# Attention's q and k projected transposed, with halves exchanged by ScalarE, and V summed out of a double-width product

## The chip, the cores and the metric

The kernel runs on one core of a Trainium2 chip. A core has five engines that work side by side, each through its own list of instructions in order: TensorE (PE: matrix products and transposes into PSUM, a memory of eight banks), VectorE (DVE), ScalarE (ACT), GpSimd (POOL) and SyncE (SP, which issues transfers). They wait for one another by semaphores. The metric is the device time of one execution in microseconds (us).

## The reference

A "macaron" layer over x, 8 batches of 1024 rows of 128 values: half a feed-forward, attention, half a feed-forward. The feed-forward is a mixture of 16 experts. The change lies in attention:

```python
    x = x + 0.5 * _L0_ffn_ref(_layernorm(x, axis=-1), ...)
    x = x + _L0_attn_ref(_layernorm(x, axis=-1), w_q, w_k, w_v)
    x = x + 0.5 * _L0_ffn_ref(_layernorm(x, axis=-1), ...)

def _rotate(t, cos, sin):
    te = t[..., 0::2]
    to = t[..., 1::2]
    re = te * cos + to * sin
    ro = -te * sin + to * cos
    return jnp.stack((re, ro), axis=-1).reshape(t.shape)

def _L0_attn_ref(x, w_q, w_k, w_v):
    q = jnp.einsum('bmd,ed->bme', x, w_q)
    ...
    q_rot = _rotate(q, cos, sin)
    k_rot = _rotate(k, cos, sin)
    scores = jnp.einsum('bqd,bkd->bqk', q_rot, k_rot) / jnp.sqrt(d)
    scores = jnp.where(causal[None], scores, -jnp.inf)
    attn = jax.nn.softmax(scores, axis=-1)
    return jnp.einsum('bqk,bkd->bqd', attn, v)
```

## The kernel before

**Precision.** Most products are taken in the type fp32r, and for them an operand is split into a high part (`_h`, a copy that rounds) and a low part (`_l`, value minus high part), and three products are added: high x high, high x low, low x high (`mm3`). The product of the probabilities with V is in plain fp32 and shows as two instructions for each block of 128 x 128.

**Stages.** Each feed-forward runs over 16 tiles of 512 rows; in a tile, `j` counts 9 units, each with two `mm3` (gate and up) and, three units later, a down product. POOL makes the low part of h for the down product (`low_half`, L385). Attention runs over 8 batches. A batch goes through 8 steps, one for each block of 128 rows: in step i PE issues the scores of block i+1, the product of the probabilities of block i-1 with V, and the transposes of the probabilities of block i. DVE takes the row maximum (`attn_max`), ACT the exponential (`attn_exp`, L692) and the copies of transposed probabilities, DVE adds the result to X (`attn_residual`, L1176).

**The projections of the next batch** are woven into these steps by a table, `STEP_ITEMS`. An item `xnT` transposes normalized x (ACT copies the high part xh, DVE subtracts for xl). An item `qkv` (eight in a batch, one for each 128 rows) multiplies 128 rows of x with the 384 columns of all three weights; ACT copies the product to `qkv_both`. POOL rotates q and k with rows on partitions: times cos, times sin with neighbouring columns exchanged, and their sum `rot` (L482, L473, L488), each 128x256. An item `qkT` (four in a batch) transposes two blocks of `rot` on PE (L1544); ACT copies the high part, DVE subtracts for the low one (L1158). Items use PSUM banks 5 and 7 in turn, and PE waits until the item before last has left its bank. Layer norm of the batch after next is made by DVE in steps 1 to 3 (`attn_ln`), POOL (`attn_shift`, L461 to L465) and ACT in steps 4 to 7 (`attn_xn`, L569).

**The first batch** has no attention batch before it. Its projections are woven into the last tile of the first feed-forward, tile 15, by `FIRST_STEPS` (PE), `SIN_STEPS` (POOL), `COS_STEPS` and `ADD_STEPS` (DVE), and the last of them stand behind that tile. There DVE does the cos products and the additions, POOL the sin products.

All engines follow the order in which the code is written; there is no scheduler.

## Time and profile before

| | us |
|---|---|
| median of 3 runs | 876.23 |
| lowest, highest | 875.33, 876.29 |
| profiled execution: its own time | 876.39 |
| profiled execution: span of the core | 874.6 |

The clock granted to TensorE is full (0.998 in the mean). The first feed-forward takes the span up to about 340 us, attention from there to about 555, the second feed-forward the rest. In the timelines one line is one group of instructions in a row, with its start, its length from first start to last end, and in brackets the idle time of the engine before it with the instruction that ended it. Instructions of one engine overlap, so what one costs the engine is the distance to the start of the next. For the probability transposes some records are missing.

### The profile page before, as it was taken

How to read it: one execution, taken by the hardware profiler on the slowest of the kernel's cores; microseconds unless marked ns; L12 is line 12 of the kernel's file. 1: busy time of each engine (PE TensorE's matmuls, PEld its weight loads, DVE VectorE, ACT ScalarE, POOL GpSimd, SP SyncE). 2: the span in 40 equal slices, each digit the busy share in tenths (PEclk: the TensorE clock that was granted, in tenths of full speed). 3: DMA queues.
4: the chain of work that ended last, by engine and by line, in shares of the span. 5: the costliest groups of instructions: out<-in, count | busy, mean ns of one | idle time of the engine just before them, and what ended most of it. 6: DMA issues, size and time to landing. Idle time of an engine off the chain costs nothing.

```text
span 874.6 us, 18644 instructions
## 1 busy us (share of the span) xinstructions
PE 858.0 (98%) x4602; PEld 725.2 (83%) x4602; DVE 684.9 (78%) x2124; ACT 601.5 (69%) x1255; POOL 566.0 (65%) x604
## 2 busy tenths in 40 slices
PE   8999999999999998999999999999999999999998
PEld 7788888888888876999999998788888888888886
DVE  6888888888888888565555566688888888888885
ACT  5566666666666687777787777676666666666664
POOL 6666666666666675786666872266666666666664
...
GB/s 121 177 233 112 109 111 117 127 136 133 133 120 97 99 98 1 2 1 1 1 0 0 0 0 1 99 100 120 130 137 130 133 116 109 109 111 113 129 134 85
DMA packets 58373, 80.61 MB, mean 92 GB/s; under 512 B 6497, under 2 KB 25185, under 8 KB 58081
## 3 DMA queue, kind: packets, MB, share of 16 engines
...
## 4 chain that ended last, share of the span: by engine, by line
PE 55%; DVE 3%; ACT 2%; issue 1%; POOL 0%; ACTq 0%; DVEq 0%
PE bank L1271 48%; PE bank L1580 3%; PE bank L1544 1%; PE bank L1376 1%; PE bank L1355 1%; DVE xl L1153 1%; PE bank L1533 0%; ACT xh L508 0%; ACT qkv_both L508 0%; ACT prob L692 0%; ACT xn L515 0%; ACT probT L508 0%; DVE prob L881 0%; DVE rope_c L1136 0%; PE bank L1369 0%
## 5 line engine op out<-in xcount | busy, mean ns | idle before, releaser
L385 POOL TENSOR_TENSOR h_l<-probT,h_h 128x512 fp32r<-128x512 f32 x255 | 330.8, 1297 | 206.3 <-ACT h_h L508 205.2
L508 ACT ACTIVATE h_h<-probT 128x512 fp32r<-128x512 f32 (+1 forms) x288 | 180.7, 628 | 71.5 <-DVE probT L891 67.9
L1271 PE MATMUL bank<-xh,w_h 128*128 128x512 f32 x544 | 222.9, 410 | 2.0 <-DVE prob L881 1.9
L543 ACT ACTIVATE bank<-bank 128x512 f32<-128x512 f32 x252 | 146.3, 581 | 103.4 <-PE bank L1271 98.9
L1271 PE MATMUL bank<-xh,w_l 128*128 128x512 f32 x544 | 214.9, 395 | 0.0
L881 DVE TENSOR_TENSOR prob<-bank,qkT 128x512 f32<-128x512 f32 x252 | 173.2, 687 | 51.9 <-ACT bank L543 39.0
L1271 PE MATMUL bank<-xl,w_h 128*128 128x512 f32 x544 | 213.1, 392 | 0.0
L891 DVE TENSOR_TENSOR probT<-prob,bank 128x512 f32<-128x512 f32 x256 | 174.2, 681 | 11.1 <-DVE biased L822 5.0
L1271 PEld LDWEIGHTS bank<-xh,w_l 128*128 128x128 f32 x544 | 102.4, 188 | 23.9
L1271 PEld LDWEIGHTS bank<-xh,w_h 128*128 128x128 f32 x544 | 102.7, 189 | 23.3 <-DVE prob L881 2.3
L1271 PEld LDWEIGHTS bank<-xl,w_h 128*128 128x128 f32 x544 | 102.7, 189 | 19.7
L1271 PE MATMUL bank<-h_h,w_h 128*128 128x512 f32 x288 | 117.5, 408 | 1.4 <-POOL h_h L385 0.8
L1271 PE MATMUL bank<-h_h,w_l 128*128 128x512 f32 x288 | 114.3, 397 | 0.2 <-ACT h_h L508 0.2
L1271 PE MATMUL bank<-h_l,w_h 128*128 128x512 f32 x256 | 101.4, 396 | 0.0
L508 ACT ACTIVATE probT<-bank 128x512 f32<-128x512 f32 (+2 forms) x129 | 64.7, 512 | 46.5 <-PE bank L1580 45.0
L1271 PE MATMUL bank<-qkv_both,probT 128*128 128x128 f32 x576 | 75.7, 277 | 3.7 <-ACT probT L508 2.5
L1271 PEld LDWEIGHTS bank<-qkv_both,probT 128*128 128x128 f32 x576 | 71.5, 191 | 6.0 <-DVE X L1176 2.4
L482 POOL TENSOR_TENSOR rope_c<-qkv_both,cos 128x256 f32<-128x256 f32 x56 | 41.0, 733 | 43.3 <-ACT qkv_both L508 43.3
L515 ACT ACTIVATE xn<-X,neg_shift,rstd 128x128 f32 (+1 forms) x128 | 61.2, 485 | 9.2 <-POOL neg_shift L394 9.2
L1271 PEld LDWEIGHTS bank<-h_h,w_h 128*128 128x128 f32 x288 | 54.2, 188 | 15.5 <-POOL h_l L385 1.3
L1271 PE MATMUL bank<-qkT 128*128 128x512 f32 (+3 forms) x288 | 65.0, 352 | 0.0
L1271 PEld LDWEIGHTS bank<-h_h,w_l 128*128 128x128 f32 x288 | 54.4, 189 | 11.5 <-ACT h_h L508 0.6
...
## 6 DMA issues: line engine op xcount, KB each, us to landing
...
qkT<-comb_rows SPq DMA_DIRECT2D x124, 128.0 KB, 3.0
...
```

The costliest lines, as they stand in the source:

```text
L385: nc.gpsimd.tensor_tensor(lo, f, hi.bitcast(F32), ALU.subtract).then_inc(done, 1)
L482: nc.gpsimd.tensor_tensor(rope_c[s][:], qkv[p][:, n, 0:2 * D].rearrange("p (w d) -> p w d", w=2), cos[:, n, :, :], ALU.mult).then_inc(rope ...
L508: return nc.scalar.activation(dst, src, ACT.Copy)
L515: ins = nc.scalar.activation(xn[:, n, :], X[:, bass.ds(NB * Tx + n, 1), :].rearrange("p a d -> p (a d)"), ACT.Identity, bias=neg_shift[:, ...
L543: nc.scalar.activation(bank[:, G_BANK[g], :], bank[:, G_BANK[g], :], ACT.Silu).then_inc(silu_done, 1)
L881: nc.vector.tensor_tensor(weighted[j % 2], bank[:, G_BANK[(q + j) % 2], :], comb_b[q][:, j, :], ALU.mult).then_inc(weighted_done, 1)
L891: nc.vector.tensor_tensor(h[g], weighted[j % 2], bank[:, u, :], ALU.mult).then_inc(h_done, 1)
L1153: nc.vector.tensor_tensor(xl_half[n][:], bank[:, m, :], xh_half[n][:].bitcast(F32), ALU.subtract).then_inc(a_xl_done, 1)
L1271: return nc.tensor.matmul(dst, lhsT, rhs, start=start, stop=stop)
L1355: ins = nc.tensor.transpose(bank[:, T_BANK, n * P:(n + 1) * P], xn[:, n, :], ident[:])
L1376: ins = nc.tensor.transpose(bank[:, YT_BANK, n * P:(n + 1) * P], yT[:, n * P:(n + 1) * P], ident[:])
L1580: ins = nc.tensor.transpose(bank[:, probT_bank(i, c, last), a * P:(a + 1) * P], prob[s][:, k0:k0 + P], ident[:])
```

## The change

It alters how q, k and V of a batch are made.

- **q and k come out transposed.** An item `qk` (four in a batch: k and q for each half of the 1024 rows) has the weights stationary and 512 columns of transposed x moving. Columns of the weights are reordered on the host, even ones first, so that the partner of a value in the rotation is 64 partitions away. ACT copies the product to `qk_x` in two instructions of 64 rows, the halves exchanged; DVE multiplies the product in PSUM by cos, once both copies are done; POOL multiplies `qk_x` by sin and adds; ACT copies the high part out of SBUF (`attn_hi`); POOL subtracts for the low part (`rope_low`). There are no `qkT` items.
- **V is a product of its own.** An item `v` (four in a batch, 256 rows each) multiplies, for each 128 rows, xh with the high and the low weights side by side (256 columns), adds xl times the high weights to the first 128, and DVE adds the two halves (`reduce_sum`) into `v`.
- **Order.** New tables; layer norm of a batch moves: DVE makes it one batch earlier, in steps 5 to 7, and in batch 0 the one for batch 2 in step 0; POOL's `attn_shift` stands first in its batch; ACT's `attn_xn` is spread over steps 2 to 7. The two unneeded layer norms past the last batch go. Behind tile 15, four of batch 0's items stand on PE, and POOL does parts 2 and 3 of batch 0 after its feed-forward.

```diff
-STEP_ITEMS = [[("xnT", 0), ("xnT", 1), ("qkv", 0)], [("qkv", 1), ("qkv", 2), ("qkv", 3)], [("qkv", 4), ("qkv", 5)],
-              [("qkv", 6), ("qkv", 7)], [("qkT", 0), ("probT", 4)],
-              [("qkT", 1), ("probT", 5)], [("qkT", 2), ("probT", 6)], [("probT", 7), ("qkT", 3)]]
+STEP_ITEMS = [[("xnT", 0), ("xnT", 1)], [("qk", 0), ("qk", 1)], [("v", 0), ("v", 1)], [("qk", 2), ("v", 2)],
+              [("qk", 3), ("probT", 4)], [("v", 3), ("probT", 5)], [("probT", 6)], [("probT", 7)]]
+HI_STEP = {3: 0, 4: 1, 6: 2, 7: 3}
+XN_STEPS = {2: (0, 1), 3: (2,), 5: (3, 4), 6: (5,), 7: (6, 7)}
...
+FIRST_ITEMS = [[("qk", 0), ("xnT", 1)], [], [("qk", 1)], [], [], [("v", 0)], [], [], []]
+FIRST_SIN, FIRST_ADD = {2: 0, 4: 1}, {3: 0, 5: 1}
+FIRST_HI = {5: 0, 7: 1}
+FIRST_LO = {6: 0, 8: 1}
...
-                elif kind == "qkv":
-                    a, blk = n // NB, slice(n % NB * P, (n % NB + 1) * P)
+                elif kind == "qk":
+                    a, cols = n // 2, slice(D * qk_part(n), D * (qk_part(n) + 1))
                     pe.wait_ge(a_xl_done, 2 * b + a + 1)
-                    mm3(bank[:, m, 0:3 * D], xh_half[a][:, blk], xl_half[a][:, blk], wqkv_h[:], wqkv_l[:]).then_inc(qkv_ready, 1)
-                else:
-                    pe.wait_ge(rot_done, QB * b + 2 * n + 2)
-                    for a in range(2):
-                        for w in range(2):
-                            c = w * 2 * P + a * P
-                            ins = nc.tensor.transpose(bank[:, m, c:c + P], rot[(2 * n + a) % ROPE_BUFS][:, w, :], ident[:])
-                    ins.then_inc(qkT_ready, 1)
+                    mm3(bank[:, m, :], wqkv_h[:, cols], wqkv_l[:, cols], xh_half[a][:], xl_half[a][:]).then_inc(qk_ready, 1)
+                else:
+                    a = n // 2
+                    pe.wait_ge(a_xl_done, 2 * b + a + 1)
+                    for t in range(2):
+                        blk, at = slice((2 * (n % 2) + t) * P, (2 * (n % 2) + t + 1) * P), 2 * D * t
+                        mm(bank[:, m, at:at + 2 * D], xh_half[a][:, blk], wv_hl, True, False)
+                        ins = mm(bank[:, m, at:at + D], xl_half[a][:, blk], wqkv_h[:, 2 * D:3 * D], False, True)
+                    ins.then_inc(v_ready, 1)
...
+                elif kind == "qk":
+                    s = n % ROPE_BUFS
+                    act.wait_ge(qk_ready, QK * b + n + 1)
+                    wait(act, rope_s_done, QK * b + n - ROPE_BUFS + 1)
+                    for a in range(2):
+                        copy(qk_x[s][a * INTER:(a + 1) * INTER, :],
+                             bank[(1 - a) * INTER:(2 - a) * INTER, m, :]).then_inc(qk_swapped, 1)
+
+            def attn_hi(n, b, p):
+
+                act.wait_ge(rot_done, QK * b + n + 1)
+                copy(qkT_h[p][:, qk_part(n), qk_cols(n)], rot[n % ROPE_BUFS][:]).then_inc(qkT_h_done, 1)
...
+                elif kind == "qk":
+                    s = n % ROPE_BUFS
+                    dve.wait_ge(qk_swapped, 2 * (QK * b + n + 1))
+                    wait(dve, rot_done, QK * b + n - ROPE_BUFS + 1)
+                    nc.vector.tensor_tensor(rope_c[s][:], bank[:, m, :], cos[:, qk_part(n), qk_cols(n)],
+                                            ALU.mult).then_inc(rope_c_done, 1)
+                elif kind == "v":
+                    dve.wait_ge(v_ready, QK * b + n + 1)
+                    nc.vector.reduce_sum(v[p][:, 2 * n:2 * n + 2, :],
+                                         bank[:, m, :].rearrange("p (n a d) -> p n d a", n=2, a=2), AX_X).then_inc(v_done, 1)
...
+                    if first and i == 0:
+                        attn_ln(2, 0)
+                        attn_ln(2, 1)
+                        attn_stats(2)
+                        dve.wait_ge(a_neg_shift_done, 2)
+                        attn_ln(2, 2)
+                    if i >= QB - 3 and ahead:
+                        attn_ln(b + 3, i - (QB - 3))
...
+            def attn_prep(b, p, last=False):
+
+                if not last:
+                    attn_shift(b + 1, rstd, neg_shift)
+                rope_sin(b, 0)
+                rope_add(b, 0)
+                rope_sin(b, 1)
+                rope_add(b, 1)
+                rope_low(b, p, 0)
+                rope_low(b, p, 1)
...
             ffn(0)
+            for n in range(2, QK):
+                rope_sin(0, n)
+                rope_add(0, n)
+            for n in range(2, QK):
+                rope_low(0, 0, n)
```

Three places in the engines' lists. First ACT in steps 1 and 2 of an attention batch (batch 0, where the loop is written out; `stage` holds `qk_x`). Before:

```order
L508 ACTIVATE qkv_both<-bank 128x384 [waits qkv_ready]
L508 ACTIVATE probT1<-bank 128x256 [waits probT_ready]
L508 ACTIVATE qkv_both<-bank 128x384 [waits qkv_ready]
L692 ACTIVATE prob0,rowsum0<-bank,negmax0 128x384 [waits probT_ready,negmax_done]
L508 ACTIVATE qkv_both<-bank 128x384 [waits qkv_ready] x2
L508 ACTIVATE probT0<-bank 128x384 [waits pv_ready,probT_ready]
L508 ACTIVATE qkv_both<-bank 128x384 [waits qkv_ready]
L692 ACTIVATE prob1,rowsum0<-bank,negmax1 128x512 [waits probT_ready,negmax_done]
L508 ACTIVATE qkv_both<-bank 128x384 [waits qkv_ready]
```

and now, up to the end of step 2, where `qkT0<-rot` is `attn_hi` for batch 0's own parts 2 and 3:

```order
L530 ACTIVATE probT1<-bank 128x256 [waits probT_ready]
L530 ACTIVATE stage<-bank 64x512 [waits rope_s_done,qk_ready]
L530 ACTIVATE stage<-bank 64x512
L720 ACTIVATE prob0,rowsum0<-bank,negmax0 128x384 [waits probT_ready,negmax_done]
L530 ACTIVATE stage<-bank 64x512 [waits rope_s_done,qk_ready]
L530 ACTIVATE stage<-bank 64x512
L530 ACTIVATE qkT0<-rot0 128x512 [waits rot_done]
L530 ACTIVATE probT0<-bank 128x384 [waits pv_ready,probT_ready]
L720 ACTIVATE prob1,rowsum0<-bank,negmax1 128x512 [waits probT_ready,negmax_done]
L530 ACTIVATE qkT0<-rot1 128x512 [waits rot_done]
```

Five copies of `qkv_both` have become four of 64 rows, two ahead of the exponential and two behind it, and in batch 0 the two high parts stand behind each exponential.

Second DVE from step 0 to step 1 of batch 0 (L1165 was, and L1187 is, the row maximum). Before:

```order
L1165 ISA bank,negmax1<-bank,mask 128x256 [waits scores_ready]
L1165 ISA negmax1 128x1
L1153 TENSOR_TENSOR xl2<-bank,xh2 128x512 [waits a_xh_done]
L1153 TENSOR_TENSOR xl0<-bank,xh0 128x512 [waits a_xh_done]
L1170 RECIPROCAL rrow0<-rowsum0 128x1 [waits exp_done,scores_ready]
L1165 ISA bank,negmax0<-bank,mask 128x384
L1165 ISA negmax0 128x1
L1176 SCALAR_TENSOR_TENSOR X<-bank,rrow0,X 128x128 [waits pv_ready,rrow_done]
L767 BN_STATS stats<-X 128x6 x4
L1170 RECIPROCAL rrow0<-rowsum0 128x1 [waits exp_done,scores_ready]
```

and now:

```order
L1187 ISA bank,negmax1<-bank,mask 128x256 [waits scores_ready]
L1187 ISA negmax1 128x1
L1170 TENSOR_TENSOR xl2<-bank,xh2 128x512 [waits a_xh_done]
L1170 TENSOR_TENSOR xl0<-bank,xh0 128x512 [waits a_xh_done]
L799 BN_STATS stats<-X 128x6 x8
L804 BN_AGGR mv<-stats 128x2 [waits a_neg_shift_done,a_stats_done]
L804 BN_AGGR mv<-stats 128x2 x7
L807 TENSOR_SCALAR var_eps<-mv 128x8 [waits a_mv_done]
L1192 RECIPROCAL rrow0<-rowsum0 128x1 [waits exp_done,scores_ready]
L1187 ISA bank,negmax0<-bank,mask 128x384
L1187 ISA negmax0 128x1
L1198 SCALAR_TENSOR_TENSOR X<-bank,rrow0,X 128x128 [waits pv_ready,rrow_done]
```

Sixteen instructions and the variance of a layer norm now stand ahead of the maximum `negmax0` of step 1; four statistics stood behind it.

Third POOL from the end of tile 15 on. Before, up to its last instruction in the tile:

```order
L473 TENSOR_TENSOR rope_s0<-qkv_both,sin 128x256 [waits rot_done,qkv_done]
L385 TENSOR_TENSOR h_l0<-probT1,h_h0 128x512 [waits h_hi_done]
L473 TENSOR_TENSOR rope_s1<-qkv_both,sin 128x256 [waits rot_done,qkv_done]
L473 TENSOR_TENSOR rope_s2<-qkv_both,sin 128x256 [waits rot_done,qkv_done]
L385 TENSOR_TENSOR h_l1<-probT0,h_h1 128x512 [waits h_hi_done]
L473 TENSOR_TENSOR rope_s3<-qkv_both,sin 128x256 [waits rot_done,qkv_done]
L385 TENSOR_TENSOR h_h2<-probT1,h_h2 64x512 [waits h_hi_done,rope_s_done,h_lo_done]
```

and now, on into attention:

```order
L390 TENSOR_TENSOR h_l2<-probT0,h_h2 128x512 [waits h_hi_done]
L390 TENSOR_TENSOR h_l0<-probT1,h_h0 128x512 [waits h_hi_done]
L390 TENSOR_TENSOR h_l1<-probT0,h_h1 128x512 [waits h_hi_done]
L390 TENSOR_TENSOR h_h2<-probT1,h_h2 64x512 [waits h_hi_done,rot_done,h_lo_done]
L481 TENSOR_TENSOR rope_s0<-stage,sin 128x512 [waits rot_done,qk_swapped,h_lo_done]
L489 TENSOR_TENSOR rot0<-rope_c0,rope_s0 128x512 [waits qkT_l_done,rope_s_done,rope_c_done]
L481 TENSOR_TENSOR rope_s1<-stage,sin 128x512 [waits rot_done,qk_swapped]
L489 TENSOR_TENSOR rot1<-rope_c1,rope_s1 128x512 [waits qkT_l_done,rope_s_done,rope_c_done]
L390 TENSOR_TENSOR qkT0<-rot0,qkT0 128x512 [waits qkT_h_done]
L390 TENSOR_TENSOR qkT0<-rot1,qkT0 128x512 [waits qkT_h_done]
```

The sin products between the last low halves are gone from there, and behind them stand six instructions for batch 0 that read `stage`, `rope_c` and the high parts.

## Rows read from the trace of the kernel before

**Rows 1.** The page, part 1: busy us, share of span, instructions.
```profile
PE 858.0 (98%) x4602; PEld 725.2 (83%) x4602; DVE 684.9 (78%) x2124; ACT 601.5 (69%) x1255; POOL 566.0 (65%) x604
```

**Rows 2.** Busy us by stretch: start:end, length, then each engine (instructions), clock, DMA.
```profile
312.67:339.54 26.87, 25.92 (x124) 21.17 (x123) 24.76 (x47) 21.44 (x43) 21.36 (x22) 1.00 0.26 72
346.87:373.14 26.27, 26.17 (x194) 24.69 (x194) 15.30 (x55) 20.22 (x50) 18.92 (x27) 1.00 0.01 2
373.14:399.68 26.54, 26.30 (x193) 24.57 (x192) 15.82 (x55) 20.49 (x51) 18.95 (x27) 1.00 0.01 2
```

**Rows 3.** Timeline of PE in batch 1 and 2: start us, length us, engine, line, operation, count.
```profile
402.89 0.86 PE L1271 MATMUL bank<-qkT 128*128 128x512 f32 x3
403.58 0.60 PE L1271 MATMUL bank<-qkv_both,probT 128*128 128x128 f32 x4
...
404.70 0.34 PE L1271 MATMUL bank<-wqkv_h,xl 128*128 128x384 f32 x1
404.88 0.34 PE L1271 MATMUL bank<-wqkv_h,xh 128*128 128x384 f32 x1
...
405.42 1.14 PE L1271 MATMUL bank<-qkT 128*128 128x512 f32 x6
406.39 0.88 PE L1271 MATMUL bank<-qkv_both,probT 128*128 128x128 f32 x6
...
408.59 1.19 PE L1271 MATMUL bank<-qkT 128*128 128x512 f32 x6
409.62 1.05 PE L1271 MATMUL bank<-qkv_both,probT 128*128 128x128 f32 x8
410.51 0.60 PE L1580 MATMUL bank<-ident,prob 128*128 128x128 f32 x4
410.95 0.60 PE L1544 MATMUL bank<-ident,rot 128*128 128x128 f32 x4
```

**Rows 4.** Timeline of ACT, same columns: tile 15's end, then batch 2.
```profile
336.22 0.59 ACT L546 ACTIVATE prob<-bank 64x512 f32<-64x512 f32 x1
...
428.33 0.49 ACT L508 ACTIVATE qkv_both<-bank 128x384 f32<-128x384 f32 x1 [0.48 <-PE bank L1271]
428.72 0.58 ACT L692 ACTIVATE prob<-bank,negmax 128x384 f32<-128x384 f32 x1
...
438.26 0.59 ACT L508 ACTIVATE qkT<-bank 128x512 fp32r<-128x512 f32 x1
438.74 0.28 ACT L508 ACTIVATE probT<-bank 128x128 f32<-128x128 f32 x1
```

**Rows 5.** Groups of POOL over the span: shape, count, busy us, mean ns, idle before, releaser.
```profile
L385 POOL TENSOR_TENSOR h_l<-probT,h_h 128x512 fp32r<-128x512 f32 x255 | 330.8, 1297 | 206.3 <-ACT h_h L508 205.2 <-DVE rot L1146 1.0
...
L488 POOL TENSOR_TENSOR rot<-rope_c,rope_s 128x256 f32<-128x256 f32 x56 | 41.0, 733 | 9.0 <-POOL rope_s L473 4.0
...
L462 POOL TENSOR_TENSOR rstd<-var_eps,neg_half 128x8 f32<-128x8 f32 x9 | 14.8, 1644 | 0.0
```

**Rows 6.** Timeline of DVE in batch 2, and in batch 7.
```profile
428.17 0.86 DVE L767 BATCH_NORM_STATS2 stats<-X 128x6 f32 x4
...
434.49 0.64 DVE L772 BATCH_NORM_AGGREGATE mv<-stats 128x2 f32<-128x6 f32 x8
435.17 0.39 DVE L775 TENSOR_SCALAR var_eps<-mv 128x8 f32<-128x8 f32 x1
...
438.89 0.69 DVE L1158 TENSOR_TENSOR qkT<-bank,qkT 128x512 fp32r<-128x512 f32 x1 [1.02 <-ACT qkT L508]
...
541.11 0.29 DVE L792 TENSOR_REDUCE bank<-bank 128x64 f32<-128x128 f32 x1
```

**Rows 7.** Timeline of PE from tile 15's end; in brackets idle before, releaser.
```profile
338.74 0.50 PE L1271 MATMUL bank<-h_h,w_h 128*128 128x512 f32 x1 [0.65 <-POOL h_l L385]
...
341.20 0.50 PE L1271 MATMUL bank<-h_h,w_h 128*128 128x512 f32 x1 [0.75 <-POOL h_h L385]
...
346.87 0.68 PE L1271 MATMUL bank<-qkT 128*128 128x384 f32 x3
```

262 lines of the change are left out of this document (126 added, 136 removed).

## The prediction

> **What bounds the kernel now.** I read the engine table first. TensorE (PE) is busy 98% of the span and the next engine, DVE, 78% [rows 1]. So a PE saving is worth its full size unless something else comes last. The second view is busy time by stretch [rows 2]. It separates the two places that the change touches. One is the last tile of the first feed-forward, tile 15 (26.87 us, with DVE busy 24.76 and PE 25.92). The other is the attention batch: 26.27 us for batch 0 and 26.54 us for batch 1, from the start of scores(2) of one batch to that of the next. In batch 1 PE is busy 26.30 of 26.54 us, ACT 20.49, POOL 18.95 and DVE 15.82. Since matmul records overlap, I count PE by the distance between starts instead, in the third view [rows 3].
>
> **PE prices** [rows 3]. Three 512-column products: 403.58 - 402.89 = 0.69, so 0.23 each. One of 384: 404.88 - 404.70 = 0.18. Scores of 512+128 columns: 0.97 (405.42 to 406.39), which leaves 0.28 for three of 128 columns, 0.09 each. Scores of 512+256: 1.03, so 0.11 for one of 256 columns. Four transposes: 410.95 - 410.51 = 0.44. Eight instructions of the probability product: 0.89, 0.11 each.
>
> **PE, the sum for a batch.** Before: eight q/k/v products of three 384-column matmuls, 24 x 0.177 = 4.25, and 16 transposes of q and k, 4 x 0.44 = 1.75; 6.0 us. After: four q/k products of three 512-column matmuls, 4 x 0.69 = 2.76, and four V products of two 256 and two 128, 4 x (0.23 + 0.20) = 1.7; 4.5 us. The columns are the same, 9216; the transposes go. PE saves 1.5 us of about 25.3 us of work in a batch; so 1.2 of the 26.54 us are waits now, and 23.8 us of work is left. The 128-column V products are the narrowest piece; their price is between 0.09 (above) and 0.11 (a transpose), and I take 0.10.
>
> The Trainium skill, page "TensorE: Matmul & The Clock Gate", section "Back-to-back issue gap", gives 81 ns for a sustained 128-column product and 131 ns for one of 512. The rows disagree on the wide one (230 ns). By its narrow figure PE would save another 0.15 us in a batch, an estimate that the sum does without.
>
> **The other engines, for a batch.** ACT gives up eight 384-column copies (428.72 - 428.33 = 0.39 each) and four 512-column ones (438.74 - 438.26 = 0.48): 5.1 us. It gets eight copies of 64 rows x 512 columns and four whole ones out of SBUF. A 64-row instruction lasts 0.59 against 0.59 to 0.60 for 128 rows [rows 4], so half the rows cost the full price: 12 x 0.49 = 5.9. Net +0.8, ACT 21.3 of 25.5 us. What a copy costs whose output rows are others than its input rows no row shows. Bounds: not under 0.4 and, if the crossing cost a second pass, 1.0; I take 0.49, as the row with the same shape. POOL gives up 24 x 0.733 = 17.6 and gets twelve of 512 elements at 1.3 [rows 5]: 15.6. DVE gives up four 0.69 and gets four cos products of the same size and four reductions of 512 inputs. A reduction of 128 inputs takes 0.29 and a 512-element instruction from PSUM 0.69 [rows 6]; I take 0.7, so +2.8, DVE 18.6. None becomes the bound by busy time. What matters is the order.
>
> **The lockstep in steps 1 and 2.** DVE's cos product waits until ACT has swapped both halves, and DVE then stands still; behind it stand the maximum of the next row block, the residual and V's additions. Zero is the start of product qk0. PE: qk0 to 0.69, qk1 to 1.38, scores(3) to 2.07, the product of step 1 to 2.5. ACT: qk0 is ready at 0.9, swaps 0.9 to 1.9 (done 2.0), exp(2) 1.9 to 2.5, the swaps of qk1 2.5 to 3.5 (done 3.55). PE takes the transposes of step 2 from 2.6 to 2.9 and v0 to 3.35. v1 needs the bank of qk1, so cos1: DVE 3.6 to 4.3. PE idles 3.35 to 4.3, one microsecond, then v1 and scores(4). Before, scores(4) starts 405.42 - 399.68 = 5.74 after scores(2) [rows 2, 3]; after, 0.97 + 4.33 + 0.43 = 5.73. The 0.95 us of PE work saved up to there is lost again.
>
> The rest of the batch is kept: steps 3 to 7 have no q/k transposes. ACT's hi copies stand behind exp and have 2 us or more of cover, and POOL's chain for parts 2 and 3 ends at about 26 in batch time, 3 us before the next batch's first swap. Two small waits are new: probT(6) is copied 0.2 us too late for step 7 since no transposes lie between, and in step 0 the copy xh stands behind xn, xn and hi on ACT, so residual(7) on DVE, and with it the next product, comes 0.45 later. Waits after: 1.0 + 0.1 + 0.2 + 0.4 = 1.7. Period 23.8 + 1.7 = 25.5 instead of 26.54. There are six such periods (scores(2) of batch 1 to that of batch 7): 6 x 1.05 = **6.3 us won**.
>
> The Trainium skill says why cos may not run beside the swap: page "PSUM — Partial Sum Buffer", section "PSUM bank collisions raise a hardware error", two engines may not touch one bank's same rows at once. No run here shows it.
>
> **Tile 15.** PE loses eight 0.53 products and two groups of transposes (0.44 each) and gets two 0.69 and one 0.43: 5.1 - 1.8 = 3.3 us less in the tile. DVE, which is 24.76 of 26.87 us busy there, loses eight cos products and eight additions. POOL's sines were late for the last two down products, where PE waited 0.65 and 0.75 [rows 7]. They now stand at j = 2 to 5, four instructions of 1.3 where 0.73 stood, which may hold up h for about 0.5. Behind the tile four products (2.7 us with v1) are new, and v3 waits for cos of qk3, which waits for ACT's swaps behind exp and yT: 1.2 us of new waits. Zero is now the last gate product of the tile, which comes the 3.3 us earlier. Its way through silu, h, high part and POOL's low part ends at 3.7, down(8) and scores(1) at 4.7; ACT swaps qk2 at 3.9 to 4.9, DVE's cos frees the bank of qk3 at 5.7, qk3 and y end at 6.9, ACT's swaps of qk3 at 7.7, cos at 8.4, v3 at 8.9, both xnT at 10.2, and scores(2) starts at 10.2. Before, that distance is about 10.9 (336.0 to 346.87 [rows 7]). So 3.3 + 0.7, less the 0.5: **3.5 won**. Bounds 2 and 5.
>
> **Batch 0 pays.** DVE now does all of layer norm for batch 2 in its step 0, ahead of the maximum of row block 2: eight statistics (2 x 0.86), eight aggregates (0.64), the variance (0.39), 2.8 us [rows 6], and exp(2) is 2.4 us late. Then POOL: parts 2 and 3 of batch 0's own q and k are finished by POOL; low2 needs hi2, which ACT does behind the swaps of step 1, low3 needs hi3, behind exp(3) in step 2. That is exp(3) at +8.4 after scores(2), hi3 to +9.5, low3 +9.7 to +11.0, and scores(4), which reads them, waits until then instead of starting at 5.73: 5.3 us lost. POOL's shift, 1.64 of it the power [rows 5], and sin0 then come just too late for ACT: 0.3. Against the 0.8 by which a plain batch is shorter than batch 0 before (26.27 to 25.5): **4.8 lost**, bounds 3 and 7.
>
> **Sum.** -6.3 - 3.5 + 4.8 = -5.0. The profiled execution took 876.39, so 871.4; by the median, 876.23, it is 871.2. The last batch has no projection and the second feed-forward is untouched, so the shift reaches the end whole.
>
> **Rivals.** (1) PE alone decides: the waits close up, 8 x 1.5 = 12 us, 864.2. For it: PE is 98% busy; against: cos1 is a chain of ACT and DVE instructions with nothing to fill it. (2) The gain is given back: batch 0 costs 6.5, the period is 25.9: tile 15 wins only 3.0: -3.8 - 3.0 + 6.5 = -0.3, 875.9. For it: the chain ACT, DVE, PE passes four swaps and two cos, and 0.1 on each is the 0.4. (3) Slower, by the swaps: crossing rows costs 0.9 instead of 0.49 for a copy. The chain up to cos1 holds four copies, so the period grows by 1.6 to 27.1, 6 x 0.6 = 3.6 lost, batch 0 and the tail 2 more: 3.6 + 2 - 3.5 + 4.8 = 6.9, 883.1. It decides from a copy of 0.75 (1.05 / 4 = 0.26 more). Against: ACT goes through the elements of a row, and 64 rows cost what 128 do. (4) The edit does not do what it says, say TensorE reads the 128-column tail slower: at 0.2 each, 8 x 0.1 = 0.8 in a batch, but half of it falls into the waits: 873.6.
>
> **Chances.** Forecast with its own range (868.5 to 874) 0.52; (1) and what lies between 0.12; (4) 0.06; (2) 0.18; (3) and smaller forms of it 0.12. The range of 8 in 10: 865.0 to 877.5. A measurement tells 0.2% (1.75 us) from no change: faster 0.70, same 0.16, slower 0.14.
>
> **What would show it.** The distance of scores(2) starts in batches 2 to 6: 25.5. PE idle before v1, released by DVE's rope_c, about 1 us each batch. The 64-row copies: 0.6 long, 0.5 apart. The reductions 0.7. In batch 0 one long PE wait of about 3 us before scores(4), released by POOL's low half. Tile 15 under 24 us. Wrong would be a swap over 0.75, a 128-column product over 0.15, or a POOL instruction over 1.5.

## The result, and the profile after

The changed kernel takes 886.00 us (median of 4 runs, 885.03 to 886.62) against 875.78 for the kernel before in the same session (875.25 to 876.29): a ratio of 1.0116, interval 1.0104 to 1.0128. It is slower by 1.2%. The forecast was 871.2 us, faster, with a range up to 877.5: wrong in sign and outside the range. The profiled execution has a span of 884.4 us against 874.6, so 9.8 us are to be explained, and 14.8 against the forecast.

The page of after, part 1 (busy us, share of the span, instructions), and busy time by stretch in the columns of [rows 2]: tile 15 (from its first gate product to its last down product but one, as in [rows 2]), batch 0 (from scores(2) to scores(2)), batch 1, batch 3.

```profile
PE 852.2 (96%) x4506; PEld 713.4 (81%) x4506; DVE 693.6 (78%) x2125; ACT 613.0 (69%) x1247; POOL 558.2 (63%) x519
```

```profile
311.52:338.60 27.08, 23.61 (x102) 18.14 (x101) 18.97 (x37) 20.95 (x40) 21.57 (x19) 0.97 0.30 72
346.96:380.88 33.92, 28.85 (x184) 25.85 (x182) 20.68 (x75) 22.83 (x53) 18.54 (x17) 0.85 0.00 1
380.88:408.28 27.40, 25.15 (x183) 22.85 (x182) 18.00 (x60) 22.98 (x53) 17.70 (x16) 1.00 0.00 1
435.07:461.88 26.81, 25.16 (x183) 22.85 (x182) 17.95 (x60) 22.53 (x51) 17.21 (x16) 1.00 0.00 0
```

Against [rows 1] and [rows 2] the reader sees PE less busy, as intended (25.16 instead of 26.30 us in a batch, 23.61 instead of 25.92 in tile 15), and no stretch shorter in return. PE has waits now that it did not have: 1.65 us in a plain batch, where batch 1 of before has 0.24, and 5.1 in batch 0, where before has 0.1.

The start of scores(2) in each batch is a ruler for the span. In us, from the timelines of PE (the mean is over the four periods between batches 2 and 6; "rest" runs to the end of the span):

| kernel | batch 0 starts | 0 to 1 | 1 to 2 | mean period | 6 to 7 | rest |
|---|---|---|---|---|---|---|
| before | 346.87 | 26.20 | 26.61 | 26.58 | 24.75 | 343.9 |
| forecast | 343.4 | 31.0 | 25.5 | 25.5 | 25.5 | 343.9 |
| after | 346.96 | 33.92 | 27.40 | 26.78 | 26.07 | 342.9 |

After less before: +0.1 up to batch 0, +7.7 in batch 0, +0.8 in batch 1, +0.8 in the four plain periods, +1.3 in batch 6 (whose period runs on into batch 7), -0.9 behind it: 9.8.

**A plain batch.** PE in batch 3 of after, from scores(2) to scores(4):

```profile
435.07 0.77 PE L1300 MATMUL bank<-qkT 128*128 128x384 f32 x3
436.11 0.48 PE L1300 MATMUL bank<-stage,probT 128*128 128x128 f32 x2 [0.27 <-DVE X L1198]
...
436.57 0.48 PE L1300 MATMUL bank<-xh,wqkv 128*128 128x512 f32 x1
...
439.59 0.55 PE L1613 MATMUL bank<-ident,prob 128*128 128x128 f32 x3 [0.26 <-ACT prob L720]
...
441.55 0.39 PE L1300 MATMUL bank<-wqkv,xh 128*128 128x256 f32 x1 [1.00 <-DVE rope_c L1176]
...
442.06 1.19 PE L1300 MATMUL bank<-qkT 128*128 128x512 f32 x6
```

The wait before v1 that the forecast named is there with its size, 1.00 us, released by DVE's `rope_c`. But scores(4) starts 442.06 - 435.07 = 6.99 us after scores(2), where 5.73 was forecast and 5.74 is what before has. From scores(4) to the next scores(2) it is 461.88 - 442.06 = 19.82; the forecast's figure is 25.5 - 5.73 = 19.77. So the whole miss of a plain period, 1.3 us, lies in these two steps. ACT in the same stretch shows its largest part (`stage` is `qk_x`; x2 is a pair of 64-row copies):

```profile
437.62 1.21 ACT L530 ACTIVATE stage<-bank 64x512 f32<-64x512 f32 x2 [0.31 <-PE bank L1300]
438.86 0.58 ACT L720 ACTIVATE prob<-bank,negmax 128x384 f32<-128x384 f32 x1
439.34 0.19 ACT L720 ACTIVATION_READ_ACCUMULATOR prob<-bank,negmax 128x1 f32 x1
439.56 1.21 ACT L530 ACTIVATE stage<-bank 64x512 f32<-64x512 f32 x2
440.79 0.49 ACT L530 ACTIVATE probT<-bank 128x384 f32<-128x384 f32 x1
```

A pair takes 1.24 us to the start of the next instruction, not 0.98. Each copy is 0.59 us long, as the row of a 64-row silu had it [rows 4], but they don't overlap as that one did.

The prices of the other new instructions, groups of after between 380 and 540 us (count, then busy us and mean ns of one):

```profile
L390 POOL TENSOR_TENSOR qkT<-rot,qkT 128x512 fp32r<-128x512 f32 x24 | 30.9, 1287 | 47.5 <-ACT qkT L530 47.4
L530 ACT ACTIVATE stage<-bank 64x512 f32<-64x512 f32 x48 | 28.4, 592 | 3.7 <-PE bank L1300 2.0
L1176 DVE TENSOR_TENSOR rope_c<-bank,cos 128x512 f32<-128x512 f32 x24 | 16.6, 692 | 31.0 <-ACT stage L530 31.0
L1180 DVE TENSOR_REDUCE stage<-bank 128x256 f32<-128x512 f32 x24 | 15.9, 684 | 1.6 <-PE bank L1300 1.6
```

DVE's cos product waits for ACT 31.0 us in 24 times, 1.3 each, and DVE stands still in them.

**Batch 0.** PE's waits, then three stretches in the columns of [rows 2]; the clock is the last number but two.

```profile
352.12 0.71 PE L1300 MATMUL bank<-stage,probT 128*128 128x128 f32 x4 [1.60 <-DVE X L1198]
354.58 0.58 PE L1300 MATMUL bank<-wqkv,xh 128*128 128x256 f32 x1 [1.00 <-DVE rope_c L1176]
357.97 2.18 PE L1300 MATMUL bank<-qkT 128*128 128x512 f32 x6 [2.28 <-POOL qkT L390]
```

```profile
350.00:355.00 5.00, 2.40 (x16) 1.82 (x15) 3.77 (x19) 2.99 (x7) 0.47 (x1) 0.92 0.00 0
355.00:360.00 5.00, 2.72 (x11) 2.25 (x10) 1.65 (x5) 1.30 (x3) 4.00 (x5) 0.50 0.01 3
360.00:365.00 5.00, 5.00 (x21) 4.62 (x21) 1.34 (x5) 1.83 (x4) 4.73 (x5) 0.56 0.00 0
```

scores(4) starts 357.97 - 346.96 = 11.01 us after scores(2), and the forecast had 11.0, for its two reasons. What it did not have stands in the clock: after PE was busy for 2.40 of 5 us the granted clock is 0.50, the lower of its two levels (1.2 instead of 2.4 GHz), and 0.56 in the next 5; from 365 on it is 1.00 again. The same six products last 2.18 us, against 1.19 in batch 3. From scores(4) on to the next scores(2), batch 0 takes 380.88 - 357.97 = 22.91 us, a plain batch 19.82. That is 3.1 more.

**Tile 15 and its end.** PE, with one line each of DVE and POOL from the same stretch:

```profile
331.53 1.34 DVE L795 TENSOR_TENSOR qkT<-rot,qkT 128x512 fp32r<-128x512 f32 x1
...
335.40 1.70 POOL L390 TENSOR_TENSOR h_l<-probT,h_h 128x512 fp32r<-128x512 f32 x1 [1.27 <-ACT h_h L530]
```

```profile
334.19 0.50 PE L1300 MATMUL bank<-h_h,w_h 128*128 128x512 f32 x1 [0.44 <-POOL h_l L390]
...
337.16 0.80 PE L1300 MATMUL bank<-h_h,w_h 128*128 128x512 f32 x1 [2.01 <-POOL h_l L390]
...
341.45 0.51 PE L1300 MATMUL bank<-qkT 128*128 128x256 f32 x3
...
345.10 0.39 PE L1300 MATMUL bank<-wqkv,xh 128*128 128x256 f32 x1 [1.18 <-DVE rope_c L1176]
```

PE reaches its last gate product earlier than before, and then waits 2.01 us for the low part of h, where before has a wait of 0.65 and, one down product later, another of 0.75 [rows 7]. The next products run at the lower clock (0.64 between 336 and 340 us; the first lasts 0.80 instead of 0.50). From the last silu of the tile, of 64 rows, to scores(2) of batch 0 it is 13.87 us (333.09 to 346.96), before 10.65 (336.22, [rows 4], to 346.87). The start of batch 0 alone hides that: the first silu of this kind, in the first tile, is at 34.24 us in before and at 33.12 in after, and over all kernels of the study it is at either 33.1 to 33.2 or 34.1 to 34.4, with the same code up to there. So of the "+0.1 up to batch 0" the change made +1.2, and this execution began 1.1 better.

### The profile page after: what moved, and what is told of

Same layout as the page of the kernel before. It is cut to its first block, busy times and chain, and to the rows that moved or that the text cites. A ratio compares the mean times of both kernels' runs of the same rounds, so it can differ in the third digit from the quotient of the medians.

```text
span 884.4 us, 18064 instructions
## 1 busy us (share of the span) xinstructions
PE 852.2 (96%) x4506; PEld 713.4 (81%) x4506; DVE 693.6 (78%) x2125; ACT 613.0 (69%) x1247; POOL 558.2 (63%) x519
## 4 chain that ended last, share of the span: by engine, by line
PE 50%; ACT 6%; issue 3%; DVE 3%; POOL 1%; ACTq 0%; DVEq 0%; POOLq 0%
PE bank L1300 45%; PE bank L1613 3%; ACT stage L530 1%; ACT prob L720 1%; PE bank L1384 1%; PE bank L1405 1%; ACT xn L591 1%; ACT probT L530 1%; ACT qkT L530 1%; DVE rope_c L1176 1%; ACT xh L530 1%; ACT xn L537 0%; POOL qkT L390 0%; DVE probT L923 0%; DVE X L1198 0%
## 5 line engine op out<-in xcount | busy, mean ns | idle before, releaser
L1300 PE MATMUL bank<-stage,probT 128*128 128x128 f32 x576 | 77.6, 280 | 7.2 <-DVE X L1198 4.1
L1300 PEld LDWEIGHTS bank<-stage,probT 128*128 128x128 f32 x576 | 71.6, 193 | 12.9 <-issue 5.7
L390 POOL TENSOR_TENSOR qkT<-rot,qkT 128x512 fp32r<-128x512 f32 x30 | 38.6, 1285 | 61.6 <-ACT qkT L530 61.6
L1300 PE MATMUL bank<-qkT 128*128 128x512 f32 (+3 forms) x288 | 67.8, 363 | 2.3 <-POOL qkT L390 2.3
```

What stands on the lines that cost most here:

```text
L390: nc.gpsimd.tensor_tensor(lo, f, hi.bitcast(F32), ALU.subtract).then_inc(done, 1)
L1300: return nc.tensor.matmul(dst, lhsT, rhs, start=start, stop=stop)
```

## The experiments

All of them are edits of the changed kernel. The columns are those of the table above, with one more, "tail": from the silu of 64 rows in tile 15, its last, to scores(2) of batch 0. It is 10.65 us in before and 13.87 in after. The ratio is against the kernel before in the same session. e4, e5, e11, e13 and e14 leave out the exchange: they show what it costs in time, and don't compute the layer. The distances of a kernel come from one execution.

| kernel | tail | batch 0 starts | 0 to 1 | 1 to 2 | mean period | 6 to 7 | median us | ratio (interval) |
|---|---|---|---|---|---|---|---|---|
| e1_ln | 12.62 | 345.75 | 31.47 | 27.40 | 26.78 | 26.08 | 883.49 | 1.0095 (1.0078-1.0111) |
| e2_hi | 13.53 | 347.84 | 29.61 | 27.40 | 26.77 | 26.06 | 882.61 | 1.0072 (1.0055-1.0089) |
| e3_ln_hi | 13.66 | 347.81 | 26.77 | 27.40 | 26.77 | 26.06 | 880.00 | 1.0046 (1.0030-1.0063) |
| e7_lo_late | 12.12 | 346.50 | 33.43 | 27.41 | 26.80 | 26.07 | 884.77 | 1.0098 (1.0081-1.0114) |
| e4_one_copy | 12.99 | 345.25 | 32.57 | 25.69 | 25.06 | 24.35 | 871.78 | 0.9959 (0.9945-0.9974) |
| e5_same_rows | 13.91 | 347.93 | 33.63 | 27.26 | 26.65 | 25.91 | 885.42 | 1.0110 (1.0093-1.0127) |
| e6_table | 13.60 | 348.04 | 32.44 | 26.60 | 25.98 | 25.26 | 881.16 | 1.0056 (1.0037-1.0076) |
| e8_all | 13.15 | 346.33 | 25.96 | 26.57 | 25.96 | 25.25 | 872.95 | 0.9971 (0.9960-0.9983) |
| e9_split | 13.73 | 348.23 | 32.56 | 26.14 | 25.60 | 24.93 | 879.57 | 1.0049 (1.0033-1.0066) |
| e10_all_split | 14.90 | 349.21 | 25.60 | 25.54 | 24.93 | 24.18 | 868.79 | 0.9913 (0.9897-0.9930) |
| e11_all_one | 11.04 | 343.28 | 24.62 | 25.44 | 24.86 | 24.17 | 862.55 | 0.9851 (0.9835-0.9867) |
| e12_split_late | 12.11 | 345.24 | 24.94 | 25.52 | 24.93 | 24.18 | 865.65 | 0.9887 (0.9870-0.9903) |
| e13_low_twice | 13.13 | 346.90 | 32.00 | 26.57 | 25.95 | 25.24 | 878.83 | 1.0034 (1.0021-1.0046) |
| e14_high_twice | 12.35 | 345.33 | 32.28 | 26.97 | 26.35 | 25.64 | 881.44 | 1.0068 (1.0051-1.0084) |

### Batch 0: the layer norm and the high parts (e1, e2, e3)

e1_ln takes DVE's layer norm for batch 2 out of step 0 of batch 0 and puts it into tile 15:

```
@@ DVE, ffn tile 15
+                if j in (2, 4):
+                    attn_ln(2, (j - 2) // 2)
+                if j == 5:
+                    attn_stats(2)
+                    dve.wait_ge(a_neg_shift_done, 2)
+                    attn_ln(2, 2)
@@ DVE, batch 0
-                    if first and i == 0:
-                        attn_ln(2, 0)
...
```

> Base is the changed kernel (886.0). Only DVE's layer norm of batch 2 is moved from step 0 of batch 0 into tile 15 (j = 2, 4, 5), where DVE is busy 17.8 of 26.9 us. Theory 1 (order: the layer norm stands ahead of the row maximum of block 2, and its 2.5 us run through exp(2), exp(3), hi3 and low3 to scores(4)): TensorE's wait of 1.6 us before the probability product of step 1 goes, batch 0 is 2.4 us shorter, 883.6. Theory 2 (the clock: most of the 7.7 us that batch 0 loses is TensorE at half clock between 355 and 365 us, set off by the waits; with a shorter wait in front the clock does not fall): 4 to 6 us, 880 to 882. Rival (scores(4) waits for POOL's low3, whose time hangs on hi3 alone, not on the layer norm): under 0.7 us.

e2_hi lets ACT make both high parts of batch 0 in step 0 instead of behind the exponentials of steps 1 and 2:

```
-                    if isinstance(b, int) and b == 0 and i in (1, 2):
-                        attn_hi(i + 1, 0, 0)
+                    if isinstance(b, int) and b == 0 and i == 0:
+                        attn_hi(2, 0, 0)
+                        attn_hi(3, 0, 0)
```

> Base is the changed kernel. Only ACT's high parts 2 and 3 of batch 0 are moved from behind exp(2) and exp(3) to the end of step 0. rot2 and rot3 are there at 344.2 and 347.1 us, so hi3 ends near 349 and low3 near 351.5. Theory 1 (order: low3 is the last to arrive at scores(4)): the 2.28 us wait before scores(4) goes, 0.5 to 1.0 comes back as later swaps: 1.3 to 1.8 less, 884.5. Theory 2 (clock): without the long wait the clock stays up in batch 0 and 4 to 5 us go, 881.5. Rival (v1's wait for cos of qk1 decides by itself): no change.

e3_ln_hi does both.

> Both: layer norm of batch 2 in tile 15, hi2 and hi3 in step 0. Theory 1 and 2 together: batch 0 then has only the plain batch's waits, 26.8 us from its scores(2) to those of batch 1 instead of 33.9: 7 less, 879. If the clock is a matter of its own (falling because of the waits at the end of tile 15), 3 to 4 less.

Batch 0 takes 33.92 us; 31.47 without the layer norm, 29.61 without the late high parts, 26.77 without both: a plain period. The two together are worth 7.15 us, and nothing else is special in batch 0. Of that, 4.1 us lie ahead of scores(4), which starts 6.89 us after scores(2) in e3 instead of 11.01. The other 3.0 lie behind it, where no wait was taken away (19.88 us to the next scores(2) instead of 22.91; 22.20 in e1, 21.45 in e2). They are the clock, which stays at the upper level in e3:

```profile
350.00:355.00 5.00, 3.58 (x23) 2.94 (x23) 2.71 (x10) 3.88 (x9) 4.85 (x6) 1.00 0.00 0
355.00:360.00 5.00, 5.00 (x38) 4.66 (x37) 3.30 (x9) 3.44 (x8) 4.29 (x4) 1.00 0.01 3
```

In e1 it is 0.80 from 350 to 355 us and 0.52 from 355 to 360, in e2 0.66 from 355 to 360, and in both 1.00 behind that. The time of e1 is that of its theory 1 (883.49, expected 883.6), though its clock fell; e2 lies between its two theories (882.61, for 884.5 and 881.5); e3 has 880.0 for 879. The median of e3 is 6.0 us below that of after. In the profiled executions batch 0 starts 0.85 us later in e3, since the first tile was 1.06 later (34.18 against 33.12). For that reason the distances, not the medians alone, carry the readings here.

### Tile 15: the low parts (e7)

e7_lo_late makes both low parts of batch 0, which DVE has in tile 15 at j = 6 and 8, at j = 8.

```
-                if j in FIRST_LO:
-                    n = FIRST_LO[j]
+                for n in (0, 1) if j == 8 else ():
```

> Base is the changed kernel. Only DVE's low part of q/k piece 0 in tile 15 is moved from j = 6, where it lasts 1.34 us beside POOL (0.68 for the other one), to j = 8, behind the last h. Theory A (that instruction, with both inputs in SBUF, waits for POOL and holds up h of units 7 and 8, and so the down product that waits 2.01 us): h(7) 1.3 us earlier, the wait under 1 us, the clock at 336 to 340 us (0.64 now) stays up: 1.3 to 2.0 less, 884.3. Rival (the wait stands with ACT's two high parts and POOL's low part, which come in that order anyway): under 0.5 less; scores(0,0) may then wait for the two low parts, 0.5 more.

PE's wait before the down product falls from 2.01 to 1.48 us (under 1 was expected), and the tail from 13.87 to 12.12. The low part between two links of h's chain cost 0.5; what remains of the wait is the chain itself. The other 1.2 is the clock, which stays at 1.00 between 336 and 340 us here. In e1 it does so too, with the wait at 2.00 as in after, and the tail is 12.62, 1.25 less. So whether the clock falls there is worth 1.0 to 1.3 us; it did in ten of the fifteen profiled executions with the change. The length of this wait alone doesn't decide it: after a wait of 2.00 the clock stayed up in e1, after 2.01 it fell in after; after 1.48 it stayed up in e7 and e12, and fell to 0.63 in e8, whose tail is 13.15 against 12.11 in e12. What does decide it was not settled.

### The exchange: one copy, or the same rows (e4, e5)

e4_one_copy has one copy of 128 rows in place of the pair:

```
-                    for a in range(2):
-                        copy(qk_x[s][a * INTER:(a + 1) * INTER, :],
-                             bank[(1 - a) * INTER:(2 - a) * INTER, m, :]).then_inc(qk_swapped, 1)
+                    copy(qk_x[s][:], bank[:, m, :]).then_inc(qk_swapped, 2)
```

> Base is the changed kernel. ACT's exchange is left out: one copy of 128 rows in place of two of 64, same rows in and out (so the halves are not exchanged, and the rotation is another one). Everything else stays. Theory S (the two copies, 1.21 us for a pair instead of the 0.98 assumed, stand in the chain swap, exp, swap, cos, v1 and make the wait of 1.0 us before v1): a pair is 0.6 shorter, the chain 1.2 shorter, the wait goes, the plain period falls from 26.79 to about 25.6: 7 less with batch 0, 879. Rival (the period is set by what else stands on ACT in step 7 and 0, or by TensorE's own work): under 0.3 us in a period, 884.

e5_same_rows keeps two copies of 64 rows, each onto its own rows (`bank[a * INTER:(a + 1) * INTER, m, :]`).

> Base is the changed kernel. Two copies of 64 rows as before, but from rows 0 to 63 to rows 0 to 63 and so on: the exchange alone is left out. Theory X (crossing rows is what keeps the two copies from overlapping): the pair falls from 1.21 to 1.1 or less, the period by 0.2 to 0.4. Rival (64-row instructions on different rows don't overlap in any case): no change, within 0.3 us of the changed kernel.

One copy: the period falls from 26.78 to 25.06 and the time to 871.78 (25.6 and 879 were expected), 0.4% faster than before. ACT of e4, in batch 3:

```profile
431.19 0.60 ACT L530 ACTIVATE stage<-bank 128x512 f32<-128x512 f32 x1 [0.37 <-PE bank L1298]
431.69 0.58 ACT L718 ACTIVATE prob<-bank,negmax 128x384 f32<-128x384 f32 x1
```

A copy of 128 rows is 0.50 us from the next instruction, the pair 1.24: 0.74 more, twice on the chain to cos1, so 1.5 us. scores(4) comes 5.53 us after scores(2) instead of 6.99, 1.46 less; the period gives 1.7. The wait before v1 is gone. With the same rows in and out the pair still takes 1.24 us (438.08 to 439.32) and the period is 26.65. Crossing from one half of the rows to the other costs nothing by itself; the rival that priced it so had the right sign of the result by another mechanism, and its price of 0.9 a copy was not reached.

### Why the copies don't overlap (e13, e14)

Two explanations were left: that 64-row copies never overlap the next instruction, or that two ACT instructions don't overlap whose first rows differ. Both kernels keep two copies of 64 rows, one into `qk_x` and one into a spare buffer; e13 takes rows 0-63 twice, e14 rows 64-127.

```
+                    for dst in (qk_x[s], spare[s]):
+                        copy(dst[0:INTER, :], bank[0:INTER, m, :]).then_inc(qk_swapped, 1)
```

> Leaves out the exchange and the upper half: both copies take rows 0-63 of the product, one into qk_x and one into a spare buffer; the rest is the changed kernel. If no ACT instruction overlaps another that begins at a different row (b): none here does begin elsewhere, so a copy to the next instruction is 0.50 us, the pair 1.0, the period 26.3 (two pairs on the chain, 0.25 each), the time 881-883 us. If a 64-row copy never overlaps (a): pair 1.2, period 26.65 to 26.8, 885-886 us.

> Leaves out the exchange and the lower half: both copies take rows 64-127, one into qk_x and one into a spare buffer. By (b) the second copy overlaps the first (they are 0.50 us apart), and the exponential behind them does not (0.61): pair 1.11 us, and the copy behind a 128-row instruction does not overlap that one; period 26.5, 883-885 us. By (a): pair 1.2, period 26.65 to 26.8, 885-886 us.

ACT of e13, and then of e14, in steps 1 and 2 of batch 3:

```profile
433.98 0.59 ACT L531 ACTIVATE stage<-bank 64x512 f32<-64x512 f32 x1 [0.31 <-PE bank L1300]
434.48 0.58 ACT L531 ACTIVATE spare<-bank 64x512 f32<-64x512 f32 x1
434.96 0.57 ACT L720 ACTIVATE prob<-bank,negmax 128x384 f32<-128x384 f32 x1
435.42 0.20 ACT L720 ACTIVATION_READ_ACCUMULATOR prob<-bank,negmax 128x1 f32 x1
435.51 0.58 ACT L531 ACTIVATE stage<-bank 64x512 f32<-64x512 f32 x1
```

```profile
433.50 0.59 ACT L531 ACTIVATE stage<-bank 64x512 f32<-64x512 f32 x1 [0.31 <-PE bank L1300]
434.00 0.58 ACT L531 ACTIVATE spare<-bank 64x512 f32<-64x512 f32 x1
434.60 0.58 ACT L720 ACTIVATE prob<-bank,negmax 128x384 f32<-128x384 f32 x1
435.08 0.20 ACT L720 ACTIVATION_READ_ACCUMULATOR prob<-bank,negmax 128x1 f32 x1
435.30 0.59 ACT L531 ACTIVATE stage<-bank 64x512 f32<-64x512 f32 x1
```

All on rows from 0 up (e13): 0.50 and 0.48 to the next. On rows 64-127: the second copy comes 0.50 behind the first, but the exponential, which begins at row 0, 0.60 behind the second. And where a copy from row 64 follows an instruction at row 0, it comes 0.22 behind the accumulator's read (435.08 to 435.30) instead of 0.09 (435.42 to 435.51). It is the change of the first row that ends the overlap, about 0.1 us each time, and an exchange pays it up to three times: going into the pair, within it, going out of it. e5 fits: its first copy begins at row 0, and comes 0.09 behind the accumulator's read (439.80 to 439.89), its second does not. On the way to cos1, from the first copy, which comes after idle time, to the last, after has four such changes (within the first pair, out of it, into the second, within the second), e5 three, e14 two and e13 none. scores(4) comes 6.99, 6.84, 6.71 and 6.43 us after scores(2): 0.14 for each change. The periods are 26.78, 26.65, 26.35 and 25.95. So 0.3 of the 0.8 us between after and e13 lies behind scores(4), where the other two pairs of a batch stand; on which wait there was not followed up. Both runs gained more than was expected of them (26.5 and 26.3).

The Trainium skill, page "VectorE: DVE Perf Modes", section "Two Vector instructions with no wait between them", has this rule for VectorE, as a model: an instruction is held until the earlier ones have finished if its input or output begins in another quarter of the rows than the last access to that memory. The runs show the like on ScalarE, between row 0 and row 64; quarters in between were not tried. The Trainium skill, page "ScalarE: Activation LUTs", section "What ACT_TABLE_LOAD costs", says that consecutive ACTIVATEs overlap by about 93 ns; e13 agrees (0.59 long, 0.50 apart), the exchange does not.

### Taking the chain apart: the table (e6)

e6_table makes q/k and V products alternate in steps 1 and 2, so that a V product lies between the two exchanges:

```
-[("qk", 0), ("qk", 1)], [("v", 0), ("v", 1)]
+[("qk", 0), ("v", 0)], [("qk", 1), ("v", 1)]
```

> Base is the changed kernel. Only the table: step 1 takes qk0 and v0, step 2 qk1 and v1, so that q/k products use bank 5 and V products bank 7, and one pair of swaps stands in each step instead of two in step 1. Theory O (the loss in the plain batch is the order: two swap pairs and two cos in one step, DVE standing between them): the wait before v1 goes and exp(2) to exp(3) come 1.2 us earlier; the period falls from 26.79 to 25.5 to 25.9, 879 to 880 in all. Rival (ACT as such is too full in steps 0 to 4): the wait moves to another step, period 26.5, 884 to 885.

The period is 25.98 and the time 881.16, just above what was expected (25.9 and 880). PE no longer waits for `rope_c`; in its place stands a wait of 0.49 us for the exponential, which is behind the exchange on ACT:

```profile
437.60 0.55 PE L1613 MATMUL bank<-ident,prob 128*128 128x128 f32 x3 [0.49 <-ACT prob L720]
```

### The exchange split between two engines (e9)

ACT makes one half, and DVE the other, ahead of its cos product, with a semaphore of its own:

```
@@ ACT
-                    for a in range(2):
-                        ...
+                    copy(qk_x[s][0:INTER, :], bank[INTER:P, m, :]).then_inc(qk_swapped, 1)
@@ DVE, ahead of the wait for qk_swapped
+                    dve.wait_ge(qk_ready, QK * b + n + 1)
+                    wait(dve, rope_s_done, QK * b + n - ROPE_BUFS + 1)
+                    nc.vector.tensor_copy(qk_x[s][INTER:P, :], bank[0:INTER, m, :]).then_inc(qk_swapped_v, 1)
```

> Whole computation, nothing left out. Of the two 64-row copies of a q/k product ACT keeps one, and DVE makes the other ahead of its cos product, so that both run side by side. Theory (the pair of copies in a row on ACT, 1.24 us until the next instruction, is what makes the chain of steps 1 and 2 longer than forecast): each pair on the chain shrinks by about 0.5 us, PE's wait before v1 falls from 1.0 us to 0.4 or less, the period from 26.8 to 25.8-26.2, the time to 877-880 us. Rival (DVE pays: four copies of 0.6 to 0.7 us more in a batch, in the same order as the row maximum and the residual, so that what ACT gains comes back as a wait on DVE): period 26.6 or more, 883-887 us.

ACT and DVE of e9, in steps 1 and 2 of batch 3:

```profile
435.07 0.60 ACT L532 ACTIVATE stage<-bank 64x512 f32<-64x512 f32 x1 [0.32 <-PE bank L1303]
435.69 0.58 ACT L720 ACTIVATE prob<-bank,negmax 128x384 f32<-128x384 f32 x1
...
435.24 0.68 DVE L1176 COPY stage<-bank 64x512 f32<-64x512 f32 x1
435.95 0.69 DVE L1179 TENSOR_TENSOR rope_c<-bank,cos 128x512 f32<-128x512 f32 x1
```

Both halves are copied side by side out of one bank (from different rows), in 0.60 and 0.68 us. The period is 25.60, lower than the theory's own 25.8, though the wait before v1 is 0.62, where it had 0.4 or less. DVE does 20.9 instead of 17.9 us in a batch, in time in which it had stood still. The same stretch shows the first row again: the copy, which begins its output at row 64, is 0.71 from the next instruction, where cos is 0.61.

### Together (e8, e10, e11, e12)

e8_all is e3, e6 and e7 in one. e10_all_split adds e9's split. e11_all_one is e8 with e4's single copy, as a bound. e12_split_late is e10 with both copies on ACT for batch 0's own items, where DVE has much to do:

```
@@ ACT
                     copy(qk_x[s][0:INTER, :], bank[INTER:P, m, :]).then_inc(qk_swapped, 1)
+                    if prologue:
+                        copy(qk_x[s][INTER:P, :], bank[0:INTER, m, :]).then_inc(qk_swapped_v, 1)
```

> The four moves together: layer norm of batch 2 in tile 15, hi2 and hi3 in step 0, the table of alternating q/k and V items, the low part of piece 0 late. If the causes are those named and separate: batch 0 -7, six periods -6, tile 15 -1.5: 871.5, under the kernel before (875.8). If the waits overlap, half of it, 878.

> Whole computation. The version with layer norm, high parts, table and low parts moved, and the copies split between ACT and DVE as well. If the pair on ACT is still on the path there, the period falls from 25.98 to about 25.5 and the time from 873 to 869-870.5 us; if the reordered table has already taken it off the path, 872-874 us, and more than 874 if DVE's added 2.6 us per batch is on it.

> Leaves out the exchange: one copy of 128 rows for the two of 64, in the version with layer norm, high parts, table and low parts moved. It bounds what the second copy still costs there. If the pair is still on the path: period 25.1 instead of 25.98, time 865-867 us. If the table took it off: period above 25.7, time 870-872 us.

> Whole computation. As the version with everything moved and the copies split between ACT and DVE, but batch 0's own products, in tile 15 and behind it, keep both copies on ACT. In the split version scores(2) of batch 0 started at 349.2 us against 346.3 with the pair on ACT, and PE waited 1.81 instead of 1.18 us for the last cos product, since DVE has low parts, the residual and the copy before it. If DVE's copies cause that, scores(2) of batch 0 starts at 346 to 347 us again, the period stays 24.95, and the time is 2 to 3 us less than 868.8: 865.5-867. If the late start came from the fall of the clock near 340 us alone, which the pair version shows too, it stays at 348-349 and the time is 868-869.

e8: 872.95 us (871.5 if the causes were separate), 0.3% faster than before. e10: 868.79; the period goes below the expected 25.5, to 24.93, but the tail grows from 13.15 to 14.90, where PE waits 1.81 instead of 1.18 us before v3. e12 has 1.18 there again, its clock stays up, and its tail is 12.11: 865.65 us, ratio 0.9887 (0.9870 to 0.9903). It computes everything, and is 1.1% faster than the kernel before and 2.3% faster than the changed one (865.65 / 886.00 = 0.977, from two sessions whose medians of before are 876.16 and 875.78). A plain batch of e12:

```profile
445.64:470.56 24.92, 24.59 (x184) 22.75 (x182) 20.86 (x64) 20.17 (x47) 17.24 (x16) 1.00 0.00 0
```

PE is busy 24.59 of 24.92 us: bound by PE again. The bound e11, without the second copy, has 24.86 for the period, so the exchange costs a batch 0.07 us there. Its time, 862.55, is below the 865 to 867 expected, with a clock of 1.00 from 336 to 340 us; of its lead over e12 of 3.1 us in the median 1.1 is in the tail (11.04), and 0.3 in batch 0.

## Why the prediction was wrong, point by point

The miss is 14.8 us. By the ruler: 3.6 up to batch 0 (-3.5 forecast, +0.1 measured), 2.9 in batch 0 (+4.8, +7.7), 9.2 in the six periods (-6.3, +2.9), and 0.9 the other way behind them. No single step makes it: a copy of the exchange costs more than was taken from the row (5.0 us in the six periods), batch 0 runs in part at the lower clock (3.1), the end of tile 15 takes longer, with waits for h and a lower clock behind them (3.9), and smaller steps have the rest.

- **PE prices.** Right enough. 1.1 us less busy time in a batch by the rows of after, forecast 1.5 by starts. A V product behind a wait is 0.51 from its start to the next instead of 0.43 (441.55 to 442.06). Rival (4) is out.
- **DVE and POOL prices.** Right: cos 0.69, reduction 0.68 (taken as 0.7), POOL 1.27 to 1.29 (1.3).
- **The swap copy: the largest step that failed.** "Half the rows cost the full price: 12 x 0.49", from the row of a 64-row silu. That instruction begins at row 0 like its neighbours and overlaps them (the next one starts 0.49 behind it); the exchange's copies don't. Measured: 0.61 to 0.62 a copy and 0.13 more in front of the first. In the lockstep of steps 1 and 2 ("swaps 0.9 to 1.9, exp, the swaps of qk1 2.5 to 3.5") that is 0.4 us for the pairs, of the second only the step within it, and 0.1 in front of the second: 0.56 by the distance from scores(2) to scores(4) (6.99, and 6.43 in e13). e13 measures the whole: without the change of rows the six periods take 155.6 instead of 160.6 us, 5.0 of the 9.2. e13, whose copies cost what was forecast, still takes 878.8, 1.0034 (1.0021 to 1.0046): this step alone doesn't make the sign, the others below do their part. The threshold ("it decides from a copy of 0.75") was too high, since it was reckoned against a sum with other errors.
- **The head of the lockstep.** The forecast let qk0 start 0.97 after scores(2), a distance taken from another step. Measured 1.50 (436.57 - 435.07): scores(2) and the transposes take longer than that, and PE waits 0.27 for the residual, which DVE has behind `xl` (the forecast has that wait, with 0.4, in the sum of the period, but not in the lockstep). In e13 it is 1.49, and scores(4) comes 6.43 after scores(2), 0.70 more than forecast; the rest of the period is 19.5, 0.25 less than forecast, and so the period (25.95) misses 25.5 by 0.45. With this and the 0.6 us that batch 1 takes above the others in every kernel with the change (PE waits 0.86 us for the residual there, not 0.27), e13's six periods are 2.6 us above the forecast, 2.6 of the 9.2.
- **"Six such periods" of 26.54.** The last of them was 24.75 in the kernel before already, as the timeline of PE showed in before; the items of batch 7's first steps fall away there. 1.6 of the 9.2 is this slip. (The 0.9 won behind batch 7 was not forecast either.)
- **The wait before v1, the waits of steps 3 to 7.** Right: 1.00 us, and 19.82 against 19.77.
- **Batch 0.** The chain to scores(4) is right to 0.01 us (11.01), and not by luck: POOL's last low part runs from 9.70 to 10.96, forecast 9.7 to 11.0, and e1 and e2 confirm both causes. Left out: what two waits of 1.6 and 2.3 us do to the clock. 3.1 us (22.91 against 19.82 behind scores(4)), shown by the products at half speed, and by e3, where clock and waits are gone together. That the clock fell because of the waits is what the order of the two rows shows, and e1 to e3 agree: with fewer waits it falls for a shorter time, with the fewest not at all. What the same waits cost in batch 0 at full clock no run shows.
- **Tile 15.** Measured from the first tile, its last silu comes 2.0 us earlier than before (299.97 against 301.98 us behind the first of its kind), where 3.3 - 0.5 = 2.8 was forecast: PE waits 1.02 us for `xl` ahead of qk1 (at 320.08 us), a wait not in the forecast. Then the tail: 13.87 us where before has 10.65, and 0.7 less than before was forecast, so 3.9 missed. Its second part, from scores(1) to scores(2), took 5.51 us (341.45 to 346.96), no longer than forecast (10.2 - 4.7 = 5.5), so all of the 3.9 lies ahead of scores(1). The forecast let h's chain end at 3.7 for the last unit and looked at no unit before it. But the unit before the last was late (the slowed low part, 0.5 by e7), and with PE's filler work gone its way through DVE, ACT and POOL was bare: waits of 0.44 and 2.01 before the down products of units 6 and 7, where before has none and 0.65, with the work for q, k and v around them. (The 0.75 that before has ahead of the last down product is gone.) The 0.5 and the clock were measured; that the cover is missing is read from the order of the rows, and no run gave PE other work there. With it came the clock, 1.2. 0.8 and 3.9, less 1.1 by which this execution began better, are the 3.6.
- **Rivals.** (3) had the outcome (883.1) and its place, the exchange in the chain of four copies, but another mechanism: not crossing, but the change of the first row, at 0.12 instead of 0.41 a copy; the rest came from batch 0 and tile 15, so that its 883.1, 2.9 below the measurement, is in part luck. (1) fell: 864.2 is nearly what e12 reaches, once the chain is split over two engines and batch 0 is mended. The PE saving was real, and everything of it was waited away.
